# One more turned expert in position 0, an earlier normalisation for position 1, and spaced last state sums

## The reference, cut to what matters

```
x = x + 0.5 * moe(layernorm(x))      # "kind 0"
x = x + mamba(layernorm(x))
x = x + 0.5 * moe(layernorm(x))      # "kind 1"

moe(x): cw = softmax(x Wr) * softmax(10 * x Wg), divided by its sum + 1e-9    # 8 experts, all of them used
        out = sum over e of cw[e] * ((silu(x Wgate[e]) * (x Wup[e])) Wdown[e]) # 128 -> 512 -> 128
mamba(x): xz = x Win; conv over 4 rows; silu; dt = softplus(..); B, C = ..
          h[t] = exp(dt A) h[t-1] + dt x B[t];  y = sum over 16 states of h C[t]
          out = ((y + D x) * silu(z)) Wout
```

## Time and profile before

| | us |
|---|---|
| median of 3 runs (1241.94 to 1242.85) | 1242.63 |
| the profiled execution, its own time | 1242.78 |
| its span, first to last instruction | 1241.0 |

### The profile page before, as it was taken

How to read it: one execution, slowest core, us unless ns; L and a number is a source line. 1 busy time by engine, 2 the same in 40 slices (tenths; PEclk the granted TensorE clock), 3 DMA queues, 4 the chain that set the end, 5 groups by cost and what they waited for, 6 DMA issues and landing times.

```text
span 1241.0 us, 20186 instructions
## 1 busy us (share of the span) xinstructions
PE 1233.1 (99%) x7072; PEld 1058.0 (85%) x7072; DVE 1143.2 (92%) x1368; ACT 1003.5 (81%) x2122; POOL 447.8 (36%) x571
## 2 busy tenths in 40 slices
PE   9999999999999999999999999999999999999999
PEld 6788788888888888888888888888888888887887
DVE  6958899999999999999999999997999999978877
ACT  7678789798898898988879898797998978846664
POOL 1021134444453453453435434452444454402000
PEclk9999999999999999999999999999999999999999
DMA  7412458787788997987889797986688989932322
GB/s 227 111 26 54 104 108 173 165 170 168 162 177 166 194 186 155 201 167 168 180 182 184 167 195 161 190 182 141 128 165 169 196 170 195 182 75 43 68 52 52
DMA packets 121015, 184.84 MB, mean 149 GB/s; under 512 B 11344, under 2 KB 38096, under 8 KB 120912
## 3 DMA queue, kind: packets, MB, share of 16 engines
q0 software_dynamic: 53568, 97.54, 45.0%
q1 hardware_dynamic: 67344, 86.00, 26.2%
HBM read 83.30 MB, written 2.69 MB: 69 GB/s over the span
## 4 chain that ended last, share of the span: by engine, by line
PE 89%; DVE 4%; ACT 4%; issue 2%; DMA 1%; POOL 0%; SPq 0%; DVEq 0%; ACTq 0%; POOLq 0%
PE PS L1105 26%; PE PS L996 18%; PE PS L999 18%; PE PS L997 18%; PE PS L1101 2%; PE PS L1097 2%; PE PS L1099 2%; DVE HB L1345 1%; PE PS L1163 1%; PE PS L1148 1%; PE PS L1032 1%; DVE HL L1301 1%; PE PS L1040 1%; ACT DA L1643 1%; DMA YE<-CWD 1%
## 5 line engine op out<-in xcount | busy, mean ns | idle before, releaser
L1105 PEld LDWEIGHTS PS<-WD,HB 128*128 128x128 f32 x3200 | 393.8, 191 | 22.1 <-issue 2.0
L1105 PE MATMUL PS<-WD,HB 128*128 128x128 f32 x3200 | 395.8, 275 | 0.0
L1345 DVE TENSOR_TENSOR HB<-PS,HB 128x1024 f32<-128x1024 f32 (+1 forms) x336 | 322.7, 961 | 72.4 <-PE PS L999 56.1
L1555 ACT ACTIVATE HB<-PS 128x512 f32<-128x512 f32 x512 | 294.9, 596 | 95.7 <-PE PS L999 93.5
L1733 POOL DMA_DIRECT2D Y<-HS x252 | 222.5, 964 | 317.1 <-DMA Y<-HS 165.5
L996 PE MATMUL PS<-XH,WG 128*128 128x512 f32 x509 | 219.5, 431 | 0.3 <-ACT HB L1555 0.2
L996 PE MATMUL PS<-XH,WU 128*128 128x512 f32 x512 | 204.6, 400 | 0.5 <-DVE HB L1345 0.4
L999 PE MATMUL PS<-XH,WU 128*128 128x512 f32 x512 | 201.1, 393 | 0.0
L999 PE MATMUL PS<-XH,WG 128*128 128x512 f32 x509 | 200.8, 394 | 0.1
L997 PE MATMUL PS<-XH,WU 128*128 128x512 f32 x512 | 200.6, 392 | 0.0
L997 PE MATMUL PS<-XH,WG 128*128 128x512 f32 x509 | 199.2, 391 | 0.0
(11 more groups left out here) (164 smaller groups left out, 1573.7 us busy)
## 6 DMA issues: line engine op xcount, KB each, us to landing
BCB<-BCD SPq DMA_DIRECT2D x128, 512.0 KB, 5.2
Y<-HS POOLq DMA_DIRECT2D x252, 256.0 KB, 6.0
XT<-YE POOLq DMA_DIRECT2D x99, 256.0 KB, 5.1
YE<-CWD SPq DMA_DIRECT2D x27, 256.0 KB, 4.6
AT<-YE POOLq DMA_DIRECT2D x21, 256.0 KB, 3.3
WD<-in_L_ffn_w_down_dram SPq DMA_DIRECT2D x8, 256.0 KB, 6.2
XT<-in_L_attn_x_dram SPq DMA_DIRECT2D x7, 256.0 KB, 6.0
out_dram<-XT SPq DMA_DIRECT2D x7, 256.0 KB, 5.5
```

The lines of the kernel that those rows point to most:

```text
L1105: z = pe.matmul(part(g, j), HB[:, i % NH, j * P:(j + 1) * P], WD[:, e, c, :], start=c == 0 and j == 0, stop=c == FC - 1 and j == SUB - 1)
L1345: v.tensor_tensor(H, PS[:, NG + i % 2:NG + i % 2 + n, :], H, ALU.mult).then_inc(S["v_h"], 1)
L1555: a.activation(HB[:, i % NH, :], gate(i), ACT.Silu).then_inc(S["a_sil"], 1)
```

## The change

Expert 6 of position 0 is turned too (28 turned experts for 27). calm() takes the allowed lead as a parameter; in front of ln_sum and ln_square of the second normalisation (q == 1, the one of prep(1)) it is 3.0 instead of 1.0; p_exp's calm() stays. Between the two last state sums, and between the second and s_yz, the planner now waits until its TensorE clock has gone on by 2.0.

```diff
+CALM_FIRST = 3.0
...
+APART = 2.0
+
+TURNS = {0: range(1, 7), 1: range(1, 8), 14: range(0, 8), 15: range(0, 7)}
-TURNS = {0: range(1, 6), 1: range(1, 8), 14: range(0, 8), 15: range(0, 7)}
...
         yield from rows_of_x()
-        yield from calm()
+        yield from calm(CALM if q != 1 else CALM_FIRST)
...
             at = step("ln_sum", q, b, xn["by"], what, after=clock["pe"], a=1.6)
             yield True
-            yield from calm()
+            yield from calm(CALM if q != 1 else CALM_FIRST)
             at = step("ln_square", q, b, after=at, a=1.6, p=2.0)
...
-    def calm():
-        while clock["a"] > clock["pe"] + CALM:
+    def calm(ahead=CALM):
+        while clock["a"] > clock["pe"] + ahead:
             yield False
...
             for n in range(LAST):
                 step("s_y", n, v=1.17)
-                yield False
+                yield from until(clock["pe"] + APART)
         at = step("s_yz", t, v=1.17)
```

## The result

The changed kernel takes 1244.03 us (median of 20 runs, 1242.86 to 1250.92), the kernel before 1242.64 us in the same stretch of runs (20 runs, 1241.63 to 1243.60). The medians differ by 1.4 us, under the 2.5 us (0.2%) that the forecast took as about what can't be told from none; the forecast was 1243.7 us, on the same side of that bound. The ratio follows the means of all runs (1244.96 and 1242.65 us), on which long runs weigh: it is 1.002 with an interval of 1.0013 to 1.0027, so the change does cost something, 0.1 to 0.3%. The profiled execution took 1243.72 us at a span of 1241.9 us.

What follows compares the result with a forecast made beforehand. TensorE, busy 1233.1 of 1241.0 us, was taken as the bound. The terms -0.8 + 1.9 - 1.0 + 1.0 + 0 gave +1.1 us, so 1243.7 us, with a range of 1241.0 to 1246.0.

Steps and rivals of the forecast that it cites:

- Part 1: Position 0, slots 24 to 27: turning expert 6 shortens four slots from 2.28 to 2.08 us, -0.8 us.
- has room from slot 24 on: Position 0: VectorE has 8.9 of 20 us free at 60 to 80 us, covering expert 6's added work.
- Part 2 (a): Slots 9 and 10: ln_sum and ln_square delay expert 3's split on ScalarE, so VectorE and TensorE wait, +1.9 us.
- (b): Near 40 us: delayed VectorE no longer waits for its row of weights; TensorE's waits at 40.80 and 43.37 go, -1.0 us.
- (c): Up to slot 23: VectorE receives p_xl, p_max and a further HI, 1.7 us less 0.7 idle, +1.0 us.
- Behind position 1: Planner's clocks shift and single steps fall a slot off; hardly a wait to remove, allowed -0.5 to +1.5 us.
- The change leaves it alone: The third product's wait of 1.23 us at 160.74, where plain slots begin behind position 1, stays as it was.
- Part 3: Last state sums spaced, near 1098 us: no TensorE wait to win, 0, at most +1.2 us.
- Hidden: Rival: moved normalisation's costs and gains cancel in position 0, only expert 6's gain remains, 1241.8 us; chance 0.27.
- Behind for good: Rival: in slots 13 to 23 extra HI copies on VectorE cost 0.34 us each, up to 1246.4 us; chance 0.13.
- POOL holds VectorE up: Rival: ln_square's three POOL operations make a full VectorE wait, +1.0 on the forecast, 1244.7 us; chance 0.04.
- The exponential: p_exp's 3.0 us hole on ScalarE moves from slot 31 to 28, costs nothing, leaves no room for a 1.38 us drain.

Runs made afterwards that it cites:

- after: The profile of the changed kernel with all its edits; this execution took 1243.72 us, the median of 20 runs is 1244.03 us.
- the variant begun in iteration 24: Changed kernel, but the normalisation for position 1 (prep(1)) begins in iteration 24, beside the turned expert 6: 1246.48 us, ratio 1.0037.
- ln_square behind the split: Changed kernel with ln_square held until ScalarE has halved expert 3's up weights; ln_sum stays in iteration 8: 1242.89 us, ratio 1.0013.
- crossed profiles: Profiles of changed-kernel variants pairing early or spread normalisation steps with the work order of the kernel before or the changed one: medians 1245.07, 1242.58, 1241.57 us.
- early front: Changed kernel's early normalisation kept, later steps held so slots 60 to 445 follow the kernel before: 1245.07 us, ratio 1.0017.
- clean one: Changed kernel, position 1's normalisation steps spread, none ahead of a weight split: 1242.58 us with the kernel before's order from slot 60, 1241.57 with the changed order.
- VectorE's part late: Changed kernel with ln_t and what follows in position 1's normalisation held to 61.0 on the planner's clock: 1243.67 us, ratio 1.0019.
- the long run of the changed kernel: Changed kernel run again, nothing edited; the profiled execution took 1248.95 us, the median of those 12 runs was 1243.72 us.
- the last variant: Changed kernel with spread normalisation and one scan of tile 0 held, so the kernel before's order returns from slot 146 to 445: 1242.25 us, ratio 0.9997.

## Why the prediction was right, and where it wasn't

**Total.** +1.1 us was forecast and +1.4 measured on the medians (+0.9 between the two profiled executions, +2.3 on the means). The side of the bound and the mechanism of position 0 were right. That the median came out so near is in part luck: position 0 cost 1.75 us, not 1.1, and the order behind it, for which the sum has no term, gave some 1.2 back (up product 32 to 256). The tail, 0.9 us more on the mean, was not foreseen at all.

**Part 1**, -0.8: not measured by itself, and it can't be: turned alone, expert 6 costs 6.5 us, because the normalisation then begins behind the turned slots; added to the moved normalisation it takes 2.1 us off (3.5 to 1.4 over before), together with the order that it changes. Within the whole change, the up products of expert 6's slots follow at 2.05 to 2.08 us (71.74 and 73.79 in after) where plain ones took 2.28. VectorE carries it, as costed: 17.05 of 20 us at 60 to 80. But "has room from slot 24 on" was read from plain slots, and turning them takes the room away; the variant begun in iteration 24 shows it.

**Part 2 (a)**, +1.9: right in place, cause and size. 1.73 us of VectorE's idle, a gap of 1.89 for TensorE, and HI of slot 9 on VectorE as said. With ln_square behind the split the wait vanished.

**(b)**, -1.0: the row-of-weights wait and the waits at 40.80 and 43.37 are gone, 0.8 us of gaps. What I didn't see is that ln_x, at 40.20, is itself ahead of a split and makes VectorE wait 0.76; VectorE's lag took that in here, and didn't in the variant of ln_square, where it costs 1.48.

**(c)**, +1.0: too small. The gaps behind p_xl and p_max are 0.58 + 1.13 = 1.7 us, all that VectorE was given (the text had 1.7 and took off 0.7 of slack). VectorE does idle 0.80 us in after, at 54.71, but between p_xl and p_max and for TensorE, which the gap behind p_xl had made late, so it pays for neither. The further HI is in slot 19, not in slot 13.

**Behind position 1.** "The change leaves it alone", said of the wait of 1.23 us near 160 us, was wrong: it became 0.22 and 0.26. The forecast allowed -0.5 to +1.5 us for a shifted order; what the order of the change gave back is 1.2 us, outside that allowance. In the crossed profiles, starts taken off, up product 256 comes 0.8 us sooner with it than with the order of before behind the early front, and 1.6 behind the clean one. On the ratios it gains nothing with the early front (1.0017 for both) and 0.0005 with the clean one (1.0002 and 0.9997), within their intervals: the tail takes it back.

**Part 3**, 0: right, shown alone.

**The rivals.** *Hidden* fell with the waits at 34 to 59 us. *Behind for good* fell: ten HI instead of six in the whole span, two of them in position 0. *POOL holds VectorE up* fell. One line each, in after, and the place where the two now meet:

```profile
L1708 POOL TENSOR_TENSOR rs<-ve,mhalf x22: 1032/1890/2092, 34.3 to 1051.4; 128x4 f32<-128x4 f32 x22
```

```profile
L1303 DVE TENSOR_TENSOR HL<-HB,HI x112: 675/680/683, 22.9 to 1231.6; 128x512 fp32r<-128x512 f32 x112
```

```profile
34.31 1.04 POOL L1708 TENSOR_TENSOR rs<-ve,mhalf 128x4 f32<-128x4 f32 x1
```

```profile
304.57 1.90 POOL L1708 TENSOR_TENSOR rs<-ve,mhalf 128x4 f32<-128x4 f32 x1
305.50 1.27 DVE L1439 TENSOR_TENSOR_SCAN HS<-DA,car,HS 128x512 f32<-128x512 f32 x1
```

HL's constant 675 to 683 ns says little by itself, as only one of the 112 begins while an rs runs. Better is the first rs: VectorE's low half of the split began inside it, at 34.50, and took its usual 0.69 us, and rs took 1.04. Of the other 21, the stretched ones (up to 2.092 us, at 661.9) lie beside VectorE operations of some 1.2 us, and what VectorE began inside them kept its length, as the scan at 305.50. So where one gives way it is POOL. By the Trainium skill, page "SBUF — State Buffer", section "Who interferes with whom", whichever comes first should block the other; these rows never show it blocking VectorE.

**The exponential.** Its hole on ScalarE, now behind slot 28, is 74.61 to 77.57 = 2.96 us, the 3.0 of the earlier trace rows: two loads of 1.28 and two small operations, again without room for the drain of some 1.38 us that the Trainium skill puts on a switch (page "ScalarE: Activation LUTs", section "What ACT_TABLE_LOAD costs"). TensorE doesn't wait for it.

```profile
74.61 1.28 ACT L1550 ACT_TABLE_LOAD   x1
...
77.57 1.19 ACT L1557 ACTIVATE HB<-PS 128x512 f32<-128x512 f32 x2
```

**What stays open.** Why the early front with the order of before has runs of 1245.7 to 1246.1 us; whether every long run of the changed kernel is the wait of 306 us, as one was profiled; and what the long runs at a clock of 1.000 are (1246.43 us with ln_square behind the split, 1246.36 and 1247.62 with VectorE's part late). No variant moved POOL's sums ahead of the issue that they wait behind and left the rest alone, so that this wait makes the tail is shown for one execution only.

## What to carry to other kernels

Before a step is moved in an order shared by several engines, look at what stands right behind it on its own engine: a pass of 1.2 to 1.8 us made no gap behind a split of weights, and gaps of 1.6 to 1.9 us ahead of one in three places (34, 44 and 70 us) where VectorE had no slack. Look at the slack of the slots as the change leaves them, not as the old profile shows them, and add up the time over runs, not one: a work order can have the better median (1241.57 us) and still a quarter of its runs 3 to 4 us longer. A place to look is an engine that works in order and has urgent work behind waits for its own transfers: here they had grown from 22 to 41 us.

## What the runs showed of the hardware

Twice a TensorE wait of 3.3 and 3.6 us (gaps of 3.50 and 3.77) was followed by two stretches of 5 us with a granted clock of 0.77 to 0.89 instead of 1.00, in the long run of the changed kernel at 306 us and with expert 6 turned only at 73 us; a product of 0.40 us took 0.63 there. In the first of them the wait itself is about two thirds of the price, the clock the rest (1.7 us of 5.2). The waits of 1.7 us in after, at 36 us, and of 1.35 in the last variant, at 269 us, left the clock at 1.00. The Trainium skill, page "TensorE: Matmul & The Clock Gate", section "What's actually happening", describes a gate that halves the array's clock when it has had little to do; the rows agree with that, and give the price in this kernel.
